# The first stage of a decoder layer: short convolution and gating for two batches in one operation

## What is computed

```
z     = rmsnorm(x, pre_norm_w) @ in_proj_w.T             # 256 -> 768 channels
z_pre = causal_conv3(z, short_w) + short_b               # 3 taps for each channel
x2, x1, v = split(z_pre, 3)
xv    = x1 * v
y     = (long_conv(xv, h) + xv * D_skip) * x2
x     = layernorm(x + (y @ out_proj_w.T + x) + mlp(...))
...
```

## Time and profile before

| | |
|---|---|
| median of 3 runs (lowest, highest) | 2232.19 us (2230.71, 2239.22) |
| the profiled execution's own time | 2231.43 us |
| its span, first to last instruction | 2229.7 us |
| mean granted TensorE clock, of full speed | 0.970 |
| PE busy | 2014.4 us (90%) |
| DVE busy | 1459.4 us (65%) |
| ACT busy | 1197.0 us (54%) |
| POOL busy | 895.9 us (40%) |

### The profile page before, as it was taken

How to read it: one execution, slowest core, us unless ns; L and a number is a source line. 1 busy time by engine, 2 the same in 40 slices (tenths; PEclk the granted TensorE clock), 3 DMA queues, 4 the chain that set the end, 5 groups by cost and what they waited for, 6 DMA issues and landing times. The chain is left out here.

```text
span 2229.7 us, 39687 instructions
## 1 busy us (share of the span) xinstructions
PE 2014.4 (90%) x12896; PEld 1407.7 (63%) x12960; DVE 1459.4 (65%) x2637; ACT 1197.0 (54%) x2377; POOL 895.9 (40%) x1340
## 2 busy tenths in 40 slices
PE   6886968999999966899999999999999999977997
PEld 4665857888888854565566655666666656534554
DVE  6897444444444335777777777777777877734776
ACT  6775233444544432455665656556565565555564
POOL 3443633555555531233334333443334433332232
PEclk9999988999999978999999999999999999998999
DMA  3343011222222115344343442434433344011222
GB/s 114 120 148 135 31 47 57 77 75 75 75 75 75 47 63 125 74 99 102 78 104 72 108 102 78 100 74 103 107 80 94 75 106 100 22 61 51 91 82 69
DMA packets 104639, 188.05 MB, mean 84 GB/s; under 512 B 27816, under 2 KB 77992, under 8 KB 98344
## 3 DMA queue, kind: packets, MB, share of 16 engines
q1 hardware_dynamic: 104488, 186.14, 31.1%
HBM read 110.23 MB, written 58.79 MB: 76 GB/s over the span
## 5 line engine op out<-in xcount | busy, mean ns | idle before, releaser
L1708 DVE TENSOR_REDUCE at_mneg<-at_ps_s 128x1 f32<-128x384 f32 (+3 forms) x704 | 437.2, 635 | 107.1 <-PE at_ps_s L1346 88.3
L1481 ACT ACTIVATE at_pt<-at_ps_w 128x512 f32<-128x512 f32 x640 | 377.4, 597 | 234.9 <-PE at_ps_w L1357 234.7
L1571 POOL TENSOR_SCALAR_AFFINE_SELECT at_pt<-at_pt 128x256 f32<-128x256 f32 (+1 forms) x640 | 231.8, 365 | 576.3 <-ACT at_pt L1481 573.4
L1345 PE MATMUL at_ps_s<-at_ks,at_qs 96*128 96x128 bf16 (+3 forms) x1024 | 258.8, 306 | 36.1 <-DVE at_mneg L1708 22.3
L1357 PE MATMUL at_ps_w<-at_qs,at_ks 97*128 97x512 bf16 (+3 forms) x1024 | 243.8, 300 | 8.8 <-ACT at_pt L1481 4.8
L1345 PEld LDWEIGHTS at_ps_s<-at_ks,at_qs 96*128 96x128 bf16 x1024 | 85.9, 99 | 225.8 <-DVE at_mneg L1708 140.6
L879 POOL TENSOR_TENSOR ml_m_lo<-ml_m,ml_m_hi 128x512 fp32r<-128x512 f32 x96 | 135.4, 1417 | 196.2 <-ACT ml_m_hi L794 196.0
L1373 PE MATMUL at_ps_o<-at_pt,at_val 128*32 128x512 f32 (+3 forms) x2048 | 166.8, 444 | 9.9 <-POOL at_pt L1571 9.8
L1346 PE MATMUL at_ps_s<-at_mask,at_ident 128*128 128x128 bf16 (+1 forms) x640 | 148.0, 231 | 0.0
L819 ACT ACTIVATE ml_gl<-ml_ps_g 128x512 f32<-128x512 f32 x96 | 56.6, 590 | 167.5 <-PE ml_ps_u L127 163.7
L1357 PEld LDWEIGHTS at_ps_w<-at_qs,at_ks 97*128 97x128 bf16 x1024 | 88.4, 98 | 61.5 <-ACT at_pt L1481 15.1
(11 more groups left out here) (250 smaller groups left out, 5566.7 us busy)
## 6 DMA issues: line engine op xcount, KB each, us to landing
parts_d<-at_parts SPq DMA_DIRECT2D x64, 384.0 KB, 2.5
at_ks<-parts_d SPq DMA_DIRECT2D x192, 128.0 KB, 7.9
at_qs<-parts_d SPq DMA_DIRECT2D x32, 384.0 KB, 5.8
pj_xin<-in_x SPq DMA_DIRECT2D x16, 512.0 KB, 5.1
gate_d<-pj_zc SPq DMA_DIRECT2D x16, 512.0 KB, 2.6
xv_all<-pj_turned_xv SPq DMA_DIRECT2D x16, 512.0 KB, 4.1
ml_turned_y<-xv_all SPq DMA_DIRECT2D x16, 512.0 KB, 3.5
ml_x<-gate_d SPq DMA_DIRECT2D x16, 512.0 KB, 4.3
```

Source lines behind the costliest of these rows:

```text
L1345: pe.matmul(out[:, i, :], qs[par][0:ROWS, h, toks], ks[par][0:ROWS, h, 0:(qt + 1) * P], start=i == 0, stop=False)
L1481: act.activation(pt[u % RING][:], ps_w[u % 2][:], ACT.Exp, scale=SCALE).then_inc(exped, 1)
L1571: pool.affine_select(out=diag, in_=diag, compare_op=ALU.is_ge, fill=0.0, base=0, pattern=pattern, channel_multiplier=-1).then_inc(cut, 1)
L1708: dve.tensor_reduce(mneg[:, g, h0 % HG:h0 % HG + count, qt], view_score(ps_s[s % 2], qt, count), AX_X, ALU.max, negate=True).then_inc(maxe ...
```

## The change

Batches are now taken in eight pairs p of 2p and 2p+1, all written out, with no loop.

- The tiles of both batches are made in one bank pair `ps_z` of 2 x 512 columns, of which there are three in turn instead of six single ones. A tile is 12 matmuls. ACT's passes, DVE's taps, POOL's products and additions handle both batches in one operation.
- zc and xv exist once (for a pair) instead of by parity. x_hi and x_lo hold a pair, by parity of the pair. xin, xn, ss, ms, rstd and turned_xv are still per batch, and so are `squares`, `root`, `norm`, `turn`, `high`, `low` and the transposes.
- The fifth and the sixth tile (`SIDES = [4, 5]`) have tap 1 made by ACT as a copy and added by POOL, the addition now behind tap 0.
- SP's turn begins with both loads for two pairs ahead; placements are seven in each of the pairs 3 to 7; xv is put in place first, and x2 is stored last, behind POOL's additions.

Cut to its core:

```diff
-    SIDE = 4
-    DONE = [1, 2, 3, 4, 6, 5]
+    SIDES = [4, 5]
+    BANKS = 3
+    NPAIR = B // 2
...
-        zc = [n.sb(f"zc{i}", [P, CT, T]) for i in range(2)]
+        zc = n.sb("zc", [P, CT, 2, T])
...
-        ps_z = [n.psum(f"ps_z{i}", [P, T]) for i in range(CT)]
+        ps_z = [n.psum(f"ps_z{i}", [P, 2, T]) for i in range(BANKS)]
...
+            for p in range(NPAIR):
+                if p + 2 < NPAIR:
+                    load(2 * p + 4)
+                    load(2 * p + 5)
...
+                if p >= 3:
+                    place_filters(7 * (p - 3), min(C, 7 * (p - 2)))
+                place(2 * p)
+                place(2 * p + 1)
+                store_gate(p)
...
+            for p in range(NPAIR):
+                more = p + 1 < NPAIR
+                if more:
+                    squares(2 * p + 2)
                 for k, ct in enumerate(ORDER):
+                    bank = ps_z[(CT * p + k) % BANKS]
+                    act.wait_ge(z_ready, CT * p + k + 1)
                     if ct < KT:
+                        wait(act, x2_stored, 32 * p)
                     else:
+                        wait(act, gated, KT * (p - 1) + k // 2 + 1)
+                    act.activation(zc[:, ct], bank[:], ACT.Identity, bias=tb[:, ct:ct + 1],
                                    scale=tap[:, ct, 2:3]).then_inc(tap2_done, 1)
+                    if k in SIDES:
+                        i = SIDES.index(k)
+                        wait(act, side_added, len(SIDES) * (p - 1) + i + 1)
+                        act.activation(side[i][:], bank[:], ACT.Copy, scale=tap[:, ct, 1:2]).then_inc(side_set, 1)
+                    if more and k == 0:
+                        norm(2 * p + 2)
+                    if more and k == 1:
+                        squares(2 * p + 3)
+                    if more and k == 2:
+                        high(2 * p + 2)
+                        norm(2 * p + 3)
+                    if more and k == 4:
+                        high(2 * p + 3)
...
+            def gate(p, k):
+                pool.wait_ge(tap0_done, CT * p + 2 * k + 2)
+                wait(pool, chunked, 2 * KT * (p - 1) + 2 * (k + 1))
+                pool.tensor_tensor(xv[:, k], zc[:, KT + k], zc[:, 2 * KT + k], ALU.mult).then_inc(gated, 1)
+
+            def add_side(p, i):
+                pool.wait_ge(side_set, len(SIDES) * p + i + 1)
+                pool.wait_ge(tap0_done, CT * p + SIDES[i] + 1)
...
+            for p in range(NPAIR):
+                if p + 1 < NPAIR:
+                    root(2 * p + 2)
+                    root(2 * p + 3)
+                gate(p, 0)
...
+                gate(p, 1)
+                add_side(p, 0)
+                add_side(p, 1)
...
+                for k, ct in enumerate(ORDER):
+                    past = CT * p + k - BANKS
+                    if past >= 0:
+                        pe.wait_ge(tap0_done, past + 1)
+                    for j in range(2):
+                        if k == 0:
+                            pe.wait_ge(low_set, 2 * p + j + 1)
+                        mm = products3(...)
+                    mm.then_inc(z_ready, 1)
+                    if p + 1 < NPAIR and k in (1, 3):
+                        turn(2 * p + 2 + k // 2)
...
+                for k, ct in enumerate(ORDER):
+                    dve.wait_ge(tap2_done, CT * p + k + 1)
...
+                    if more and k == 2:
+                        low(2 * p + 2)
+                    if more and k == 4:
+                        low(2 * p + 3)
+                    if k == 3:
+                        chunk(p, 0)
+                chunk(p, 1)
```

More of the change, by code:

```diff
@@ L362, in exponents @@
                     act.activation(f.readout[:], f.readout[:], ACT.Exp).then_inc(f.exp_out, 1)
-            squares(0, 0)
-            norm(0, 0)
-            high(0, 0)
+            for b in range(2):
+                squares(b)
+                norm(b)
+                high(b)
             act.wait_ge(par_loaded, 64)
[L369 to L372, removed]
+            for p in range(NPAIR):
+                more = p + 1 < NPAIR
+                if more:
+                    squares(2 * p + 2)
@@ L381, in step @@
+                    act.activation(zc[:, ct], bank[:], ACT.Identity, bias=tb[:, ct:ct + 1],
                                    scale=tap[:, ct, 2:3]).then_inc(tap2_done, 1)
-                    if k == SIDE:
-                        wait(act, side_added, b - 1)
-                        act.activation(side[par][:], ps_z[ct][:], ACT.Copy, scale=tap[:, ct, 1:2]).then_inc(side_set, 1)
-                    if k == 1 and not last:
-                        norm(b + 1, 1 - par)
-                    if k == 3 and not last:
-                        high(b + 1, 1 - par)
@@ L444, in _, with turn @@
             pe.wait_ge(par_loaded, 64)
-            def turn(b, par):
+            def turn(b):
                 pe.wait_ge(normed, QT * (b + 1))
@@ new lines, in _, with chunk @@
+            low(0)
+            low(1)
+            def chunk(p, k):
+                if k == 0:
+                    for i in range(2):
+                        wait(dve, placed[i], 16 * p)
+                dve.wait_ge(gated, KT * p + k + 1)
+                for j in range(2):
+                    dst = turned_xv[j][:, k * C:(k + 1) * C, :].rearrange("p c n -> p n c")
+                    dve.transpose(dst, xv[:, k, j, :].rearrange("p (n c) -> p n c", c=C)).then_inc(chunked, 1)
+            direct = [k for k in range(CT) if k not in SIDES]
@@ new lines, in _ @@
+            for p in range(NPAIR):
+                more = p + 1 < NPAIR
+                for k, ct in enumerate(ORDER):
+                    bank = ps_z[(CT * p + k) % BANKS]
+                    dve.wait_ge(tap2_done, CT * p + k + 1)
+                    if k in direct:
+                        dve.scalar_tensor_tensor(zc[:, ct, :, 1:T], bank[:, :, 0:T - 1], tap[:, ct, 1:2],
+                                                 zc[:, ct, :, 1:T], ALU.mult, ALU.add).then_inc(tap1_done, 1)
+                        dve.wait_ge(tap1_done, len(direct) * p + direct.index(k) + 1)
+                    else:
+                        dve.wait_ge(side_set, len(SIDES) * p + SIDES.index(k) + 1)
+                    dve.scalar_tensor_tensor(zc[:, ct, :, 2:T], bank[:, :, 0:T - 2], tap[:, ct, 0:1],
+                                             zc[:, ct, :, 2:T], ALU.mult, ALU.add).then_inc(tap0_done, 1)
+                    if more and k == 2:
[5 more added lines that the diff above has]
+                chunk(p, 1)
+                if p == 1:
@@ L524, in step @@
                     sum_filters()
-            over_late(dve, B, step)
 def longconv(nc, f, xv_all, gw, w_out, w_gate, w_up, w_tail, w_down, w_scale, c_ident):
```

155 lines of the change are left out of this document (55 added, 100 removed).

## The result

The changed kernel takes 2270.93 us (2270.09 to 2271.31, 4 runs), the kernel before beside it 2232.13 us (2230.71 to 2239.22, 4 runs): a ratio of 1.0154, 95% interval 1.0136 to 1.0172. It is slower by 39 us, in the direction of the forecast of 2254 us (22 slower) and 3 us above the top of the range. The profiled execution has a span of 2269.6 us and a clock of 0.956 (before 2229.7 and 0.970).

A forecast was written before the change was run, and what follows sets the result against it. VectorE, busy 21.5 of 23.3 us per two batches, was taken as the bound. 2231.4 + 4.4 (start and pairs at full clock) + 17 (clock falls) = 2252.8, with the median 0.8 above: 2254 us, range 2230 to 2268.

The forecast's parts named there:

- the falls: TensorE's clock dropping to 1.2 GHz behind PE gaps ahead of turns: 10 at 1.7 us, +17 us (bounds 0 and 30).
- last pair: The final pair of the projection, without turns or norms: about 17.5 us against 21.3, -3.8.
- The chain: Queue order across the engines ties each pair together: 24.9 us per pair at full clock against 23.3, 1.6 slower.
- Both links: POOL's norm behind its second addition, and the second turn behind VectorE's low half; PE idles about 2.8 and 2.4 us.
- three in four: Share of the 13 PE gaps ahead of turns expected to drop the clock, giving 10 falls.
- The filter pairs: Second pair, with filter sums on VectorE and a filter product ahead of POOL's norm: 3.0 us of filter work, 27.9 us.
- Start: Two batches must be normalised before the first group is whole: first tap at 24 us against 18.2, +6.
- The last store: The projection's final store moves behind POOL's addition: within 0.5 us of before.
- The stages behind: Stages after the projection: the forecast added no term for them.
- The first rival: VectorE stays the bound, with POOL's norm off the path: 19.9 us per pair, about -20, 2212 us; chance 0.12.
- The loop: Unrolling the projection removes nothing visible: steps with and without a loop were read as both 23.3 us.
- the loads: Loads first in a turn, then seven placements holding the queue 9.7 us: no effect on time.

The follow-up runs named there:

- 2: Changed kernel with the norm of the batch that opens the next pair, and its squares, made a pair earlier: 2239.90 us.
- 3: Changed kernel with high and low half of the pair's first turned batch ahead of the third tile's pass and taps: 2246.06 us.
- 4: Changed kernel with both moves, norm a pair earlier and first high and low half ahead of the third tile: 2215.59 us, ratio 0.9918.
- 6: Changed kernel with the sixth tile's middle tap back on VectorE, one side tile and no second addition on POOL: 2243.95 us.
- 5: Changed kernel, order untouched, with eight and six overwritten matmuls on PE ahead of a pair's first and second turn: 2252.39 us.
- 8: Kernel before with its projection's loop written out on every engine: 2234.74 us, ratio 0.9997.
- 9: Changed kernel with one unused GpSimd product of 512 elements behind the projection's last store, to shift later stages by 1.3 us: 2268.51 us.
- 10: Changed kernel with one unused GpSimd product of 1024 elements behind the projection's last store, to shift later stages by 2.4 us: 2271.40 us.
- 11: Changed kernel with norm a pair earlier and both turned batches' high and low halves ahead of the third and fifth tiles: 2207.84 us, ratio 0.9880.
- 7: Kernel before, batch by batch, with two side tiles, the sixth tile's middle tap also by ScalarE and POOL: 2251.05 us.

## Why the forecast was right, and where it fell short

**The mechanism was right, the size too small.** On the profiled executions the forecast was 21.4 us more than before, and 39.9 were measured. Of the 18.5 us between them 10.1 lie in the projection and 8.3 in the later stages. Step by step, the forecast's pieces with their share of the falls (10 of 13 gaps at 1.7, 1.3 us a gap) against the trace:

| piece | forecast us | measured us |
|---|---|---|
| first tap | 24.2 | 26.05 |
| pair 0 | 24.8 | 25.1 |
| pair 1 (filters) | 30.5 | 33.0 |
| pair 2 | 27.5 | 28.2 |
| pairs 3 to 6 | 110.1 | 112.95 |
| last pair | 17.5 | 17.5 |
| from there to the next stage | 6.3 | 8.2 |
| next stage starts at | 240.9 | 251.0 |
| stages behind, against before | 0 | +8.3 |

- *The chain.* 24.9 us forecast; 25.3 with the gaps filled. Idle 2.8 and 2.4 forecast, 3.09 and 2.35 measured; ScalarE's wait for the norm 2.5 and 2.67. Both links are shown by their removal (2, 3, 4, 6); in these runs the buffers are as in the change, and the step fell to 20 and 19 us all the same. One inner sum doesn't close: 24.9 us less PE's 18.4 of work leave 6.5 us of idle, not the 5.2 of the two gaps. The trace has 6.07, with a third gap of 0.62 us.
- *The falls.* Their price was right: 1.7 forecast, 1.55 and 1.56 in experiments 5 and 2, and 1.7 over the four steady pairs of the change (112.95 us less four steps of 25.3, for seven falls). The bounds of 1.8 and 2.3, from the durations of the turns, were not: by the clock of the earlier trace rows (0.89 over 30.1 us, 0.94 over 27.7) all three falls before lose 1.7 each at most, so that 6 us and not 5.5 are left for filter work. Their number was too small: "three in four" came from four gaps of 2.0 to 2.7 us, and chance had its part in it, since behind the same four gaps in experiment 8 the clock fell once; in the change 12 of 13 fell, in experiments 9 and 10 11 of 13. Two more falls are 3.4 us, within the bound of 13 that I gave. What the Trainium skill (TensorE: Matmul & The Clock Gate, HAM oscillation) gives as its rule, longer gaps than these, the traces contradict: 2.35 to 3.12 us sufficed nearly every time.
- *The filter pairs.* I gave the filter work 3.0 us of the 5.5, all of it in pair 1. With the gaps filled that pair takes 30.7 against 25.3, and one fall is still in it (clock 0.94, 1.7 us at most), so the work costs 3.7 us or more there. The product on POOL ahead of the norm also makes the first gaps of pairs 1 and 2 4.97 and 4.96 us long, where I put all gaps at 2.4 to 2.8; the clock was low for longer there (0.84 and 0.82).
- *Start.* 1.9 us too little: the second turn took 1.97 instead of the 1.1 that I counted, the half group behind it 2.1 instead of 1.7, and batch 1's norm ended 0.4 us later than in the kernel before. I had priced the start at full clock; the matmuls there start every 0.43 us until 22.7.
- *The last store.* "Within 0.5 us" was wrong: the store waits for the second addition, which ends 0.7 us behind VectorE's last operation, and it is two transfers of 512 KB behind two others, which take 4.4 us to land where one took 2.6. The next stage starts 8.2 us behind VectorE's last operation instead of 6.3.
- *The stages behind.* Taken as unchanged. They took 8.3 us more, and without them the result lies at 2262.6, inside the range. The spread of the runs shown of before (2230.7 to 2239.2) held that warning, and the profiled execution is at its low end; the range should have taken in those 8 us.
- *The first rival* (VectorE's count of operations decides) needed the norm off the path. Experiments 4 and 11 are that case: with the norm and the low halves moved, the saving of the rule in the Trainium skill (VectorE: DVE Perf Modes, Rules for kernel authors) comes out, 18.2 us busy instead of 21.5 and a step of 19.1. The count of operations is only part of this saving: with one side tile VectorE is busy for 19.6 (6), so merging is worth 1.9 us and the tap handed to ScalarE and POOL most of the rest. The rule agrees with the trace on busy time, and says nothing of the order in which the work is queued.
- *The loop* costs next to nothing, as forecast, 0.16 us a step (8), though the reading behind it was wrong. No run tried *the loads* alone; PE's gaps in a steady pair are ended by ScalarE and VectorE, none by a load.

## What to carry to other kernels

When operations are merged, follow what stands behind each of them in its queue: a small one that opens the next round (here a norm of 1.4 us) must not stand behind the largest and latest of this one. Count the gaps that an order gives TensorE, and price each with the clock behind it; then move the next round's preparation ahead, before giving the merging up. And where executions of the same kernel spread by several us, put that spread into the range.

## What the runs showed of the hardware

- The granted clock fell to the 1.2 GHz level behind most gaps of 2.35 to 3.12 us, at 1.55 to 1.7 us lost each, behind both of 1.95 and 1.96 us in experiment 6, and in no steady pair behind gaps of 0.95 to 1.5 us (experiments 5 and 7). Gaps of the same length differ: 2.36 us at 158.11 in experiment 2 kept the clock, 2.38 at 134.30 lost it.
- A fall can set in some tenths of a us after work has resumed: a turn at full clock (1.06 us), then eight matmuls 0.43 us apart.
- The same instructions of the later stages took from 2010.2 to 2023.0 us in the profiled executions, 0.6%, with a lower clock in the 120 us shown above in the longest four (0.79 to 0.82) than in the shortest three (0.90).
